# A gated state-space scan on one core: both SiLU gates moved to ScalarE's Silu table, once per unit

## The chip, the cores and the metric

One core of one Trainium2 chip runs the whole program in one launch. The metric is the device time of an execution in microseconds (us). The core has five engines with in-order streams that meet at semaphores: TensorE (PE), VectorE (DVE), ScalarE (ACT), GpSimd (POOL) and SyncE (SP), which here issues the DMAs.

## What is computed

The input is an image batch (4, 512, 24, 24). After a norm over channels it is pixel-shuffled to sequences of 2304 tokens of 128 channels, a token in front, and passed through one selective state-space block. The result is added to the input; then a token norm and a routed mixture of memory tokens follow. The part that matters here:

```python
xz = einsum('bld,ed->ble', seq, in_proj_w);  u, z = split(xz, 2)
u = sum(up[:, k:k + L, :] * conv_w[:, k] for k in range(4)) + conv_b
u = silu(u)
dt, Bm, Cm = split(u @ x_proj_w.T, ...)
dt = softplus(dt @ dt_proj_w.T + dt_proj_b)
A = -exp(A_log)                       # 256 channels x 16 states
h = exp(dt_t * A) * h + (dt_t * u_t) * B_t      # for each token t
y = sum over states of h * C_t
y = (y + u * D) * silu(z)
out = y @ out_proj_w.T
```

All in float32. There are two SiLU gates: that of `u` behind the convolution, and that of `z`, which multiplies the output of the scan.

## The kernel before

Channels of the block (256) lie on 128 partitions in two halves. The sequence is cut into 6 chunks for each of 4 images: 24 **units** of 384 tokens, taken in the order chunk, image. A unit J goes through 16 **steps** `s`, one for each state of the scan. The main work of step s, spread over four engines, is

- ACT, `decay` (L525): `exp(dt * A)` for state s + 1, one activation for each half, from `DT` into the PSUM banks `DA`, where it waits until the scan of state s has read the same half (`scan_done`). There is one such pair of banks, so a decay is computed one state ahead at most;
- DVE, `drive` (L1094), for state s + 1: `dt * u * B`, or POOL in its place (L459) for states 3, 5, 7 and 9, issued two steps ahead; then the two scans of state s (L1130);
- POOL (L447): the product of state s - 1 with C;
- PE (L804): the sum over states into `Yp`, three steps behind.

Round this main work every engine has side work put at fixed steps, for the neighbouring units: in step s of unit J there is work of unit J + 1 (`front`: conv output, `U`, x_proj, softplus) and of unit J - 1 (`back`: gate `VV`, out_proj, residual, token norm, store). The order in each engine's stream is just the order of the code. Of that side work these lines matter:

- **The gate of u**, before. It is computed as `x * exp(-ln(1 + exp(-x)))`, so that all of ScalarE's functions lie in one table set, loaded once (L496): Exp of half 0 in step 15 (L535), Exp of half 1 in step 0 (L539), a clamp on POOL in step 0 (L452), Ln in step 1 (L581), Exp in step 2 (L584), and the product with the PSUM value on DVE in step 3 (L1119), which writes `U`.
- **The gate of z**, before. Exp and a copy out of PSUM (L628, L630), a clamp on POOL in step 13 (L468), Ln and Exp in steps 14 and 15 (L675, L678), and on POOL in step 1 of the next unit the product with z (L438), which writes `GZ`.
- **`VV`** (L1105), DVE, in step 3 before the drive and the scan: `Yp * GZ` of unit J - 1. PE's sum of state 0 of unit J waits for it, since it writes `Yp` anew.
- Behind it on PE, in order: that sum (step 3), x_proj (L816, step 3), in step 4 the spread of B, the next sum, out_proj (L829), the residual (L832) and a small correction (L952). ScalarE copies from these: `PART` and `XDT` (L556, L558) in step 4 ahead of the decays of state 5; `X` and `PART` (L543, L547) in step 5 ahead of the decays of state 6.

In the last three units the routing of the mixture, its gathers and its matmuls (L885) stand in further steps; their weights, eight 128 x 128 blocks for each image, lie in buffers that are free by then.

Of the kernel before, what the change touches and what calls it, by code (L numbers as in the profile page):

```python
# [69 lines left out]
def build(nc, x, tok, w_in, conv_w, conv_b, xp_w, dt_w, dt_b, a_log, dvec, op_w, mem, router, out):  # L70
    ctx = ExitStack()
    with ctx:
# [422 lines left out]
        def _(act):  # L495
# [31 lines left out]

            def step(J, par, s, main, front, back, prev, conv, norm):
# [163 lines left out]
            def prologue():  # L692
# [4 lines left out]
                act.wait_ge(conv_ready, 1)  # L697
                act.activation(SG[:, 0], PP[:, 0, 0:T], ACT.Exp, bias=NCB[:, 0:1], scale=-1.0).then_inc(gate_exp, 1)
                act.wait_ge(gate_clamped, 1)
                act.activation(SG[:, 0], SG[:, 0], ACT.Ln, bias=1.0).then_inc(gate_chain, 1)  # L700
                act.wait_ge(gate_chain, 1)
                act.activation(SG[:, 0], SG[:, 0], ACT.Exp, scale=-1.0).then_inc(gate_ready, 1)

                act.wait_ge(conv_ready, 2)
                act.activation(SG[:, 1], PP[:, 1, 0:T], ACT.Exp, bias=NCB[:, 1:2], scale=-1.0).then_inc(gate_exp, 1)
                act.wait_ge(clamped, 1)
# [573 lines left out]
```

## Time and profile before

| | |
|---|---|
| median of 3 runs | 1246.76 us (1246.51 to 1247.19) |
| profiled execution, its own time | 1244.71 us |
| its span | 1242.9 us |
| mean granted TensorE clock | 0.959 |
| busy: PE / DVE / ACT / POOL | 1069.5 / 1106.5 / 872.8 / 1103.8 us |
| scans (L1130, 768) | 728.2 us, 0.997 each |
| products with C (L447, 384) | 692.2 us, 1.820 each |
| sums (L804, 1536 passes) | 583.5 us |
| decays (L525, 768) | 431.7 us, 0.577 each |

Busy time is what an engine spent in instructions; the rest of the span it waited, and the view of the waits says for whom. A timeline row gives the start, the duration, the engine, the line and what it writes and reads; in brackets stands how long the engine had been idle before it and what ended that. Adjacent instructions of a kind are merged to one row (x2, x4). A granted clock of 1.00 is 2.4 GHz on TensorE; a stretch under that had parts at 1.2 GHz.

### The profile page before, as it was taken

Reading aid. Unit: us, or ns where it says so; the run is one execution under the profiler, and the core shown is the slowest. Engines: PE = TensorE matmul, PEld = TensorE weight load, DVE = VectorE, ACT = ScalarE, POOL = GpSimd, SP = SyncE. Lnnn points to the kernel's source line nnn. Section 1 sums busy time; section 2 is a strip of 40 time slices with the busy share of each in tenths; the row PEclk is TensorE's granted clock in tenths of the full one; section 3 lists DMA queues with packets and bytes.
Section 4 is the critical chain, followed back from the end, with each engine's and each line's share of the span. In section 5 each row is a group of like instructions: output and inputs, shape, how many; then the busy total and the mean of one; then the engine's idle time right before and its main releaser. Section 6 shows DMA issues by size and latency. Waiting matters only on the chain.

```text
span 1242.9 us, 13315 instructions
## 1 busy us (share of the span) xinstructions
PE 1069.5 (86%) x3786; PEld 621.7 (50%) x3786; DVE 1106.5 (89%) x1271; ACT 872.8 (70%) x1629; POOL 1103.8 (89%) x752
## 2 busy tenths in 40 slices
PE   6788888888889889988888898888898988877997
PEld 4455455455455555544554555545555545443454
DVE  3799998989999989999989899999899999978684
ACT  4687676776776876776767768768767777757653
POOL 4589999989999899999998899999998999959685
PEclk9799999899999999999998999999989999989899
DMA  6222132121321222221322213212212222244260
GB/s 170 102 77 103 62 105 94 67 103 60 108 104 59 97 89 77 90 103 59 108 73 88 104 59 108 97 66 91 96 64 104 89 74 102 79 148 171 98 184 26
DMA packets 64540, 116.80 MB, mean 94 GB/s; under 512 B 34219, under 2 KB 47955, under 8 KB 64467
## 3 DMA queue, kind: packets, MB, share of 16 engines
q1 hardware_dynamic: 64466, 115.96, 27.7%
q8 instruction: 30, 0.49, 0.2%
q14 instruction: 44, 0.35, 0.1%
HBM read 108.47 MB, written 7.47 MB: 93 GB/s over the span
## 4 chain that ended last, share of the span: by engine, by line
PE 32%; ACT 23%; DVE 16%; POOL 15%; issue 12%; POOLq 0%; DMA 0%; DVEq 0%; SPq 0%; ACTq 0%
PE Yp L804 13%; DVE SCAN L1130 10%; POOL SCAN L447 7%; ACT DA L525 6%; PE PP L945 5%; POOL SCAN L459 4%; DVE SCAN L1094 3%; PE PP L927 3%; PE PP L885 2%; PE PP L816 2%; ACT GATES L605 2%; ACT GATES L589 1%; ACT GATES L596 1%; ACT GATES L599 1%; ACT GATES L603 1%
## 5 line engine op out<-in xcount | busy, mean ns | idle before, releaser
L1130 DVE TENSOR_TENSOR_SCAN SCAN<-DA,CAR,SCAN 128x384 f32<-128x384 f32 x768 | 728.2, 997 | 50.1 <-ACT DA L525 30.4
L447 POOL TENSOR_TENSOR SCAN<-SCAN,CS 128x768 f32<-128x768 f32 x384 | 692.2, 1820 | 40.1 <-DVE SCAN L1130 39.2
L804 PE MATMUL Yp<-SCAN,IDENT 128*128 128x384 f32 x1536 | 583.5, 506 | 64.9 <-POOL SCAN L447 56.8
L525 ACT ACTIVATE DA<-UDT,A 128x384 f32<-128x384 f32 x768 | 431.7, 577 | 273.1 <-DVE SCAN L1130 271.0
L804 PEld LDWEIGHTS Yp<-SCAN,IDENT 128*128 128x128 f32 x1536 | 285.7, 196 | 261.8 <-POOL SCAN L447 103.9
L1094 DVE TENSOR_TENSOR SCAN<-UDT,BB 128x768 f32<-128x768 f32 x288 | 268.0, 931 | 10.1 <-PE BB L786 10.0
L459 POOL TENSOR_TENSOR SCAN<-UDT,BS 128x768 f32<-128x768 f32 x96 | 175.1, 1824 | 0.0
L945 PE MATMUL PP<-XN,WT 128*128 128x384 f32 x352 | 126.0, 490 | 7.0 <-ACT GZ L630 7.0
L786 PE MATMUL BB<-PT,SEL 96*128 96x384 bf16 x288 | 97.1, 337 | 3.7 <-DVE SCAN L1094 3.7
L945 PEld LDWEIGHTS PP<-XN,WT 128*128 128x128 f32 x352 | 64.8, 189 | 61.0 <-issue 19.9
L475 POOL TENSOR_TENSOR UDT<-UDT 128x768 f32<-128x768 f32 x23 | 41.7, 1813 | 51.9 <-DVE UDT L1177 51.9
L910 PE MATMUL PP<-SQ,MEANW 128*128 128x96 f32 x168 | 28.3, 321 | 45.3 <-ACT SQ L672 45.3
L786 PEld LDWEIGHTS BB<-PT,SEL 96*128 96x128 bf16 x288 | 30.4, 106 | 52.0 <-issue 25.6
L910 PEld LDWEIGHTS PP<-SQ,MEANW 128*128 128x128 f32 x168 | 24.3, 223 | 58.2 <-ACT SQ L672 58.2
L816 PE MATMUL PP<-UDT,XPT 128*104 128x384 f32 x92 | 43.9, 609 | 2.7 <-DVE UDT L1119 2.5
L927 PE MATMUL PP<-XN,WZT 128*128 128x384 f32 x96 | 39.3, 535 | 7.5 <-ACT LNV L620 5.5
L426 POOL TENSOR_TENSOR XN<-XC,RSTD 128x192 f32<-128x192 f32 x48 | 27.0, 587 | 20.7 <-ACT RSTD L690 20.7
L438 POOL TENSOR_TENSOR GZ<-GZ,SGZ 128x768 f32<-128x768 f32 x24 | 43.5, 1814 | 0.7 <-ACT SGZ L678 0.7
L464 POOL TENSOR_TENSOR GATES<-GATES 128x768 f32<-128x768 f32 x23 | 41.8, 1818 | 2.0 <-ACT GATES L610 2.0
L1173 DVE SCALAR_TENSOR_TENSOR GATES<-GATES 128x768 f32<-128x768 f32 x23 | 35.8, 1555 | 4.3 <-ACT GATES L616 4.3
L847 PE MATMUL PP<-SQ,MEANW 128*128 128x96 f32 x192 | 26.4, 280 | 13.7 <-ACT SQ L633 12.8
L829 PE MATMUL PP<-VV,OPT 128*128 128x192 f32 x192 | 36.9, 333 | 1.1 <-DVE VV L1105 1.1
(224 smaller groups left out, 1190.8 us busy)
## 6 DMA issues: line engine op xcount, KB each, us to landing
CS<-bc_rows SPq DMA_DIRECT2D x96, 768.0 KB, 4.1
BS<-bc_rows SPq DMA_DIRECT2D x24, 768.0 KB, 6.0
out<-XN SPq DMA_DIRECT2D x32, 192.0 KB, 2.5
X<-in_x SPq DMA_DIRECT2D x24, 192.0 KB, 3.5
X<-in_L_ffn_memory_tokens SPq DMA_DIRECT2D x16, 256.0 KB, 3.0
XN<-in_L_ffn_memory_tokens SPq DMA_DIRECT2D x16, 256.0 KB, 3.0
bc_rows<-XDT SPq DMA_DIRECT2D x24, 48.0 KB, 1.5
X<-in_L_ffn_memory_router SPq DMA_DIRECT2D x1, 512.0 KB, 3.8
```

The source lines that it names most:

```text
L438: pool.tensor_tensor(GZ[:, :, :], GZ[:, :, :], SGZ[:, :, :], ALU.mult).then_inc(gz_ready, 1)
L447: pool.tensor_tensor(M[:, n1 % MRING], HB[:, n1 % HRING], over_halves(CS[:, n1 % CRING]), ALU.mult).then_inc(m_ready, 1)
L459: pool.tensor_tensor(HB[:, n2 % HRING], DTU[:, par], over_halves(BS[:, pool_index(n2)]), ALU.mult).then_inc(dbu_pool, 1)
L525: act.activation(DA[:, h, 0:T], DT[:, par, h], ACT.Exp, scale=A[:, h, n:n + 1])\
L786: pe.matmul(BB[:, dve_index(n) % 2, 0:T], SEL[:, n], PT[:, par], start=True, stop=True)\
L804: last = pe.matmul(Yp[:, h, 0:T], IDENT[:, :], M[:, n3 % MRING, h], start=n3 == 0, stop=n3 == NS - 1)
L816: last = pe.matmul(PP[0:XROWS, 1, 0:T], XPT[:, h], U[:, fp, h], start=h == 0, stop=h == 1)
L910: last = pe.matmul(STAT, MEANW[:, :], SQ[:, q], start=q == 0, stop=q == Q - 1)
L927: last = pe.matmul(PP[:, h, 0:T], WZT[:, h], unit_seq(J), start=True, stop=True)
L945: last = pe.matmul(PP[:, h, 0:T], WT[:, h, tap], XN[:, ds((J + 2) * SLOT + tap, T)], start=tap == 0, stop=tap == TAPS - 1)
L1094: dve.tensor_tensor(HB[:, n % HRING], DTU[:, par], over_halves(BB[:, dve_index(n) % 2, 0:T]), ALU.mult)\
L1130: dve.tensor_tensor_scan(HB[:, s % HRING, h], DA[:, h, 0:T], HB[:, s % HRING, h], CAR[:, ds(J * NS * HALVES + s * HALVES + h, 1)], ALU.mul ...
```

## The change

Both gates are now one activation each, ScalarE's `Silu`. It lies in another table set than Exp and Ln, so a unit gets one excursion: in step 0, behind the decays of state 0 and ahead of those of state 1, ScalarE loads the set `silu_and_others`, computes `U` of unit J + 1 straight from the convolution's PSUM (two halves, bias in the instruction) and `GZ` of unit J - 1 from a copy `ZB`, and loads the old set again. The z of a unit is copied from PSUM once, at its old place. The clamps, the Ln and Exp passes, the product on POOL and the products on DVE go. The setup does the same once for unit 0. The code also gets a provision for decays computed ahead into SBUF (`AHEAD`, `DAS1`, `DAS2`), but `AHEAD` is the empty tuple, so all decays still go through the one pair of banks. The mixture weights of image 1, which lay in the buffer of the old gates, move to a free part of `XN`; for that ScalarE waits for the stores of the earlier units.

```diff
+AHEAD = ()
@@ step of gpsimd
-                if back and s == 1:
-                    pool.wait_ge(sgz_ready, k + 1)
-                    pool.tensor_tensor(GZ[:, :, :], GZ[:, :, :], SGZ[:, :, :], ALU.mult).then_inc(gz_ready, 1)
...
-                if front and s == 0:
-                    pool.wait_ge(sg_chain, 2 * f + 1)
-                    pool.tensor_scalar(SG[:, :, :], SG[:, :, :], EXP_LIMIT, 0.0, ALU.min, ALU.max).then_inc(clamped, 1)
...
-                if main and s == 13:
-                    pool.wait_ge(sgz_chain, 2 * J + 1)
-                    pool.tensor_scalar(SGZ[:, :, :], SGZ[:, :, :], EXP_LIMIT, 0.0, ALU.min, ALU.max).then_inc(ez_clamped, 1)
@@ step of scalar
-                if conv and s == 15:
-                    act.wait_ge(conv_ready, 2 * (J + 2) + 1)
-                    positive(act, u_ready, J + 2)
-                    act.activation(SG[:, 0], PP[:, 0, 0:T], ACT.Exp, bias=NCB[:, 0:1], scale=-1.0)
-                if front and s == 0:
-                    act.wait_ge(conv_ready, 2 * f + 2)
-                    act.activation(SG[:, 1], PP[:, 1, 0:T], ACT.Exp, bias=NCB[:, 1:2], scale=-1.0).then_inc(sg_chain, 1)
+                if s == 0 and (front or back):
+                    act.preload_act_table_set("silu_and_others")
+                    if front:
+                        act.wait_ge(conv_ready, 2 * f + 1)
+                        positive(act, ysum_done, NS * (f - 2) + 9)
+                        for h in range(HALVES):
+                            act.wait_ge(conv_ready, 2 * f + h + 1)
+                            last = act.activation(U[:, fp, h], PP[:, h, 0:T], ACT.Silu, bias=CB_[:, h:h + 1])
+                        last.then_inc(u_ready, 1)
+                    if back:
+                        act.wait_ge(z_copied, k + 1)
+                        positive(act, v_ready, k)
+                        act.activation(GZ[:, :, :], ZB[:, :, :], ACT.Silu).then_inc(gz_ready, 1)
+                    act.preload_act_table_set("natural_log_exp_and_others")
...
-                if front and s == 1:
-                    act.wait_ge(clamped, f + 1)
-                    act.activation(SG[:, :, :], SG[:, :, :], ACT.Ln, bias=1.0).then_inc(sg_chain, 1)
-                if front and s == 2:
-                    act.wait_ge(sg_chain, 2 * f + 2)
-                    act.activation(SG[:, :, :], SG[:, :, :], ACT.Exp, scale=-1.0).then_inc(sg_ready, 1)
...
-                    positive(act, gz_ready, J)
-                    act.activation(SGZ[:, :, :], PPT, ACT.Exp, scale=-1.0).then_inc(sgz_chain, 1)
-                    positive(act, v_ready, J)
-                    act.activation(GZ[:, :, :], PPT, ACT.Copy).then_inc(z_clamped, 1)
+                    act.activation(ZB[:, :, :], PPT, ACT.Copy).then_inc(z_copied, 1)
...
-                if main and s == 14:
-                    act.wait_ge(ez_clamped, J + 1)
-                    act.activation(SGZ[:, :, :], SGZ[:, :, :], ACT.Ln, bias=1.0).then_inc(sgz_chain, 1)
-                if main and s == 15:
-                    act.wait_ge(sgz_chain, 2 * J + 2)
-                    act.activation(SGZ[:, :, :], SGZ[:, :, :], ACT.Exp, scale=-1.0).then_inc(sgz_ready, 1)
@@ step of vector
-                if front and s == 3:
-                    dve.wait_ge(sg_ready, f + 1)
-                    for h in range(HALVES):
-                        last = dve.scalar_tensor_tensor(out=U[:, fp, h], in0=PP[:, h, 0:T], scalar=CB_[:, h:h + 1],
-                                                        in1=SG[:, h], op0=ALU.add, op1=ALU.mult)
-                    last.then_inc(u_ready, 1)
```

ScalarE, from the z copy of a middle unit to step 3 of the next (`DA` are decays, `SGZ` and `GATES` the old gates), before:

```order
L628 ACTIVATE SGZ<-PP 128x768
L630 ACTIVATE GZ<-PP 128x768
L525 ACTIVATE DA<-UDT,A 128x384 x2
L574 ACTIVATE CAR<-SCAN 128x8
L525 ACTIVATE DA<-UDT,A 128x384 x2
L675 ACTIVATE SGZ<-SGZ 128x768
L535 ACTIVATE GATES<-PP,minus_conv_bias 128x384
L525 ACTIVATE DA<-UDT,A 128x384 x2
L678 ACTIVATE SGZ<-SGZ 128x768
L539 ACTIVATE GATES<-PP,minus_conv_bias 128x384
L525 ACTIVATE DA<-UDT,A 128x384 x4
L574 ACTIVATE CAR<-SCAN 128x8
```

and after the change:

```order
L626 ACTIVATE ZB<-PP 128x768
L513 ACTIVATE DA<-UDT,A 128x384 x2
L579 ACTIVATE CAR<-SCAN 128x8
L513 ACTIVATE DA<-UDT,A 128x384 x4
L529 ACT_TABLE_LOAD
L535 ACTIVATE UDT<-PP,conv_bias 128x384 x2
L540 ACTIVATE GZ<-ZB 128x768
L541 ACT_TABLE_LOAD
L513 ACTIVATE DA<-UDT,A 128x384 x4
L579 ACTIVATE CAR<-SCAN 128x8
```

The side work that stood between several pairs of decays stands in one block between the decays of state 0 (the last two of the first x4) and those of state 1.

GpSimd, from the norm in step 15 to the drive of state 5, before:

```order
L429 COPY XN<-XN 128x3
L447 TENSOR_TENSOR SCAN<-SCAN,CS 128x768
L452 TENSOR_SCALAR GATES<-GATES 128x768
L438 TENSOR_TENSOR GZ<-GZ,SGZ 128x768
L447 TENSOR_TENSOR SCAN<-SCAN,CS 128x768
L459 TENSOR_TENSOR SCAN<-UDT,BS 128x768
L447 TENSOR_TENSOR SCAN<-SCAN,CS 128x768 x2
L459 TENSOR_TENSOR SCAN<-UDT,BS 128x768
```

and after:

```order
L434 COPY XN<-XN 128x3
L448 TENSOR_TENSOR SCAN<-SCAN,CS 128x768 x2
L456 TENSOR_TENSOR SCAN<-UDT,BS 128x768
L448 TENSOR_TENSOR SCAN<-SCAN,CS 128x768 x2
L456 TENSOR_TENSOR SCAN<-UDT,BS 128x768
```

Two operations ahead of the product of state 0 and the drive of state 3 are gone. PE's stream holds the same 1019 rows in both programs, and its order is that of the section above.

## Rows read from the trace of the kernel before

**Rows 1.** The page, busy time of the engines, share of the span, instructions.
```profile
PE 1069.5 (86%) x3786; PEld 621.7 (50%) x3786; DVE 1106.5 (89%) x1271; ACT 872.8 (70%) x1629; POOL 1103.8 (89%) x752
```
**Rows 2.** The waits of VectorE: us in total, times, longest.
```profile
DVE SCAN L1130 <- ACT DA L525: 30.4, 32, 1.1
DVE SCAN L1130 <- POOL SCAN L459: 19.3, 40, 0.7
```
**Rows 3.** Timeline of VectorE, `VV` in units 1 and 20: start, duration.
```profile
96.31 0.92 DVE L1105 TENSOR_TENSOR VV<-Yp,GZ 128x768 f32<-128x768 f32 x1
...
1017.37 0.92 DVE L1105 TENSOR_TENSOR VV<-Yp,GZ 128x768 f32<-128x768 f32 x1
```
**Rows 4.** Timeline of ScalarE and VectorE at the start of unit 20.
```profile
1010.30 0.58 ACT L525 ACTIVATE DA<-UDT,A 128x384 f32<-128x384 f32 x1 [0.26 <-DVE SCAN L1130]
...
1012.29 0.58 ACT L539 ACTIVATE GATES<-PP,minus_conv_bias 128x384 f32<-128x384 f32 x1 [0.64 <-PE PP L945]
1012.77 1.08 ACT L525 ACTIVATE DA<-UDT,A 128x384 f32<-128x384 f32 x2
...
1011.03 1.91 DVE L1130 TENSOR_TENSOR_SCAN SCAN<-DA,CAR,SCAN 128x384 f32<-128x384 f32 x2
...
1013.71 3.73 DVE L1130 TENSOR_TENSOR_SCAN SCAN<-DA,CAR,SCAN 128x384 f32<-128x384 f32 x4
```
**Rows 5.** Groups by line: busy us, mean ns of one, idle before.
```profile
L438 POOL TENSOR_TENSOR GZ<-GZ,SGZ 128x768 f32<-128x768 f32 x24 | 43.5, 1814 | 0.7 <-ACT SGZ L678 0.7
L1119 DVE SCALAR_TENSOR_TENSOR UDT<-PP,conv_bias,GATES 128x384 f32<-128x384 f32 x46 | 26.0, 603 | 0.6 <-ACT GATES L584 0.6
L675 ACT ACTIVATE SGZ<-SGZ 128x768 f32<-128x768 f32 x24 | 19.9, 828 | 0.0
L630 ACT ACTIVATE GZ<-PP 128x768 f32<-128x768 f32 x24 | 19.3, 804 | 0.0
```
**Rows 6.** Timeline of ScalarE at the program's start.
```profile
0.75 1.28 ACT L496 ACT_TABLE_LOAD   x1 [0.75 <-PEq L1269]
11.66 0.52 ACT L683 ACTIVATE SQ<-XC 128x384 f32<-128x384 f32 x1 [9.63 <-DVE XC L1182]
```
**Rows 7.** Timeline of unit 20, steps 3 to 5: VectorE, TensorE, ScalarE.
```profile
1020.44 3.74 DVE L1130 TENSOR_TENSOR_SCAN SCAN<-DA,CAR,SCAN 128x384 f32<-128x384 f32 x4 [0.24 <-POOL SCAN L459]
...
1025.76 3.74 DVE L1130 TENSOR_TENSOR_SCAN SCAN<-DA,CAR,SCAN 128x384 f32<-128x384 f32 x4 [0.73 <-POOL SCAN L459]
...
1018.69 1.56 PE L804 MATMUL Yp<-SCAN,IDENT 128*128 128x384 f32 x4 [2.23 <-POOL SCAN L447]
...
1023.62 1.53 PE L829 MATMUL PP<-VV,OPT 128*128 128x192 f32 x8
...
1025.84 0.49 ACT L543 ACTIVATE X<-PP 128x384 f32<-128x384 f32 x1 [0.97 <-PE PP L832]
```
**Rows 8.** Timeline of unit 12, steps 1 to 6: VectorE, TensorE, ScalarE.
```profile
625.41 3.73 DVE L1130 TENSOR_TENSOR_SCAN SCAN<-DA,CAR,SCAN 128x384 f32<-128x384 f32 x4
...
630.39 1.84 PE L804 MATMUL Yp<-SCAN,IDENT 128*128 128x384 f32 x4 [2.79 <-POOL SCAN L447]
...
632.03 2.80 PE L816 MATMUL PP<-UDT,XPT 128*104 128x384 f32 x4
...
639.22 1.08 ACT L525 ACTIVATE DA<-UDT,A 128x384 f32<-128x384 f32 x2
639.92 1.93 DVE L1130 TENSOR_TENSOR_SCAN SCAN<-DA,CAR,SCAN 128x384 f32<-128x384 f32 x2 [0.55 <-ACT DA L525]
```
**Rows 9.** Busy us by stretch, then the granted clock, DMA share and GB/s.
```profile
581.00:629.00 48.00, 41.73 (x152) 23.78 (x152) 45.07 (x51) 35.28 (x66) 45.45 (x31) 1.00 0.24 88
629.00:678.00 49.00, 43.53 (x152) 25.35 (x152) 45.48 (x53) 35.54 (x66) 45.73 (x31) 0.93 0.25 86
```
**Rows 10.** Timeline of VectorE in units 0 and 23.
```profile
48.09 3.73 DVE L1130 TENSOR_TENSOR_SCAN SCAN<-DA,CAR,SCAN 128x384 f32<-128x384 f32 x4
...
1185.90 0.96 DVE L1105 TENSOR_TENSOR VV<-Yp,GZ 128x768 f32<-128x768 f32 x1 [2.77 <-PE Yp L804]
```

More of the change, by code:

```diff
@@ L33 @@
 XP_M = XROWS
-NEG_LIMIT = -44.0
-EXP_LIMIT = 1.0e19
+AHEAD = ()
 EPS_C, EPS_T = 1e-6, 1e-5
@@ L63, in dve_index, with da_index @@
     return sum(1 for m in range(n) if m not in POOL_STATES)
+def da_index(unit, n):
+    return (NS - len(AHEAD)) * unit + (n - sum(1 for m in AHEAD if m < n))
 def pool_index(n):
@@ L96, in build @@
         GATES = sb("GATES", [P, 4 * HALVES * T])
-        SG, SE, SR, SS = (GATES[:, i * HALVES * T:(i + 1) * HALVES * T].rearrange("p (h t) -> p h t", h=HALVES)
-                          for i in range(4))
-        SGZ = sb("SGZ", [P, HALVES, T])
+        DAS1, SE, SR, SS = (GATES[:, i * HALVES * T:(i + 1) * HALVES * T].rearrange("p (h t) -> p h t", h=HALVES)
+                            for i in range(4))
+        ZB = sb("ZB", [P, HALVES, T])
+        DAS2 = sb("DAS2", [P, HALVES, T])
         GZ = sb("GZ", [P, HALVES, T])
@@ L140, in build @@
         WI = ([WT[:, i // TAPS, i % TAPS] for i in range(TOPK)],
-              [GATES[:, i * P:(i + 1) * P] for i in range(6)] + [X[:, XFREE + i * P:XFREE + (i + 1) * P] for i in range(2)],
+              [XN[:, NFREE + i * P:NFREE + (i + 1) * P] for i in range(6)] + [X[:, XFREE + i * P:XFREE + (i + 1) * P] for i in range(2)],
               [GATES[:, (8 + i) * P:(9 + i) * P] for i in range(TOPK)],
@@ L526, in decay, with decay_ahead @@
                     .then_inc(da_ready, 1)
+            def decay_ahead(J, par, i):
+                n = AHEAD[i]
+                positive(act, scan_done, 2 * (NS * (J - 1) + n + 1))
+                for h in range(HALVES):
+                    act.activation((DAS1, DAS2)[i][:, h], DT[:, par, h], ACT.Exp, scale=A[:, h, n:n + 1])\
+                        .then_inc(das_ready, 1)
             def step(J, par, s, main, front, back, prev, conv, norm):
@@ L563, in step @@
                         unit, upar, n1 = J + 1, 1 - par, 0
-                    if s < NS - 1 or front:
+                    if (s < NS - 1 or front) and n1 not in AHEAD:
                         if n1 == 0:
@@ L568, in step @@
                         decay(unit, upar, n1, N + 1, 1)
+                    if front and s >= NS - len(AHEAD):
+                        act.wait_ge(dt_ready, J + 2)
+                        decay_ahead(J + 1, 1 - par, s - NS + len(AHEAD))
                 if s % GRP == 1 and (main and s > 1 or prev and s == 1):
@@ L655, in step @@
                         act.wait_ge(f_dve, 9)
+                        if b == 1:
+                            act.wait_ge(stored, 16 * (UNITS - 3))
                         if b >= 2:
@@ L695, in prologue @@
                 weights()
[L697 to L706, printed above, removed]
-                act.activation(SG[:, 1], SG[:, 1], ACT.Ln, bias=1.0).then_inc(sg_chain, 2)
-                act.wait_ge(sg_chain, 2)
-                act.activation(SG[:, 1], SG[:, 1], ACT.Exp, scale=-1.0).then_inc(sg_ready, 1)
-                act.wait_ge(set_dve, 3)
-                act.activation(TSG, TUC, ACT.Exp, scale=-1.0).then_inc(set_act, 1)
-                act.wait_ge(set_act, 5)
-                act.activation(TSG, TSG, ACT.Ln, bias=1.0).then_inc(set_act, 1)
-                act.wait_ge(set_act, 6)
-                act.activation(TSG, TSG, ACT.Exp, scale=-1.0).then_inc(set_act, 1)
+                act.preload_act_table_set("silu_and_others")
+                for h in range(HALVES):
+                    act.wait_ge(conv_ready, h + 1)
+                    act.activation(U[:, 0, h], PP[:, h, 0:T], ACT.Silu, bias=CB_[:, h:h + 1])\
+                        .then_inc(u_ready if h else half_u, 1)
+                act.wait_ge(set_pe, 3)
+                for h in range(HALVES):
+                    last = act.activation(TU[:, h:h + 1], ST0[:, h:h + 1], ACT.Silu, bias=CB_[:, h:h + 1])
+                last.then_inc(set_act, 1)
+                act.preload_act_table_set("natural_log_exp_and_others")
                 square(1)
@@ L767, in first_main @@
                 decay(0, 0, 0, 0, 1)
-                act.wait_ge(conv_ready, 3)
-                act.wait_ge(u_ready, 1)
-                act.activation(SG[:, 0], PP[:, 0, 0:T], ACT.Exp, bias=NCB[:, 0:1], scale=-1.0)
+                for i in range(len(AHEAD)):
+                    decay_ahead(0, 0, i)
             prologue()
@@ L1091, in drive @@
                 positive(dve, m_ready, N - HRING + 1)
+                product = DA[:, :, 0:T] if n in AHEAD else HB[:, n % HRING]
                 dve.wait_ge(car_saved, 4 * BATCH + 4 * unit + (n - HRING) // GRP + 1)
                 dve.wait_ge(b_ready, NDVE * unit + dve_index(n) + 1)
-                dve.tensor_tensor(HB[:, n % HRING], DTU[:, par], over_halves(BB[:, dve_index(n) % 2, 0:T]), ALU.mult)\
+                dve.tensor_tensor(product, DTU[:, par], over_halves(BB[:, dve_index(n) % 2, 0:T]), ALU.mult)\
                     .then_inc(dbu_dve, 1)
@@ L1106, in step @@
                 if main:
-                    if s + 1 < NS and s + 1 not in POOL_STATES:
+                    if s + 1 < NS and s + 1 not in POOL_STATES and s + 1 not in AHEAD:
                         drive(J, par, s + 1, N + 1)
@@ L1128, in step @@
                     for h in range(HALVES):
-                        dve.wait_ge(da_ready, 2 * N + h + 1)
-                        dve.tensor_tensor_scan(HB[:, s % HRING, h], DA[:, h, 0:T], HB[:, s % HRING, h],
+                        if s in AHEAD:
+                            dve.wait_ge(das_ready, HALVES * (len(AHEAD) * J + AHEAD.index(s)) + h + 1)
+                            factor, term = (DAS1, DAS2)[AHEAD.index(s)][:, h], DA[:, h, 0:T]
+                        else:
+                            dve.wait_ge(da_ready, 2 * da_index(J, s) + h + 1)
+                            factor, term = DA[:, h, 0:T], HB[:, s % HRING, h]
+                        dve.tensor_tensor_scan(HB[:, s % HRING, h], factor, term,
                                                CAR[:, ds(J * NS * HALVES + s * HALVES + h, 1)],
                                                ALU.mult, ALU.add).then_inc(scan_done, 1)
+                    if s + 1 in AHEAD:
+                        dve.wait_ge(scan_done, 2 * (N + 1))
+                        drive(J, par, s + 1, N + 1)
                 if at(J, ROUTE) and s == 8:
```

74 lines of the change are left out of this document (29 added, 45 removed).

## The prediction

> **What bounds the kernel now.** I read the page first, then the waits of VectorE, the timeline of a unit, and the clock by stretches. The page shows VectorE (DVE), GpSimd (POOL) and TensorE (PE) all at 86 to 89% [rows 1]: no engine alone is full. The waits of VectorE say what fills the rest: its scans stood 30.4 us for ScalarE's decays and 19.3 us for GpSimd's products [rows 2]. So the limit is a ring in lockstep: decay (ACT), scan (DVE), product with C (POOL), sum (PE). The gate product `VV` comes once per unit; from unit 1 to unit 20 it moves from 96.31 to 1017.37, 19 units of 48.48 us [rows 3].
>
> The place that matters is a unit's first states. ScalarE ends the decays of state 0 at 1010.30 + 0.58 = 1010.88; the last Exp of the old gates starts at 1012.29 (it waits for the convolution); VectorE scans state 0 from 1011.03 and state 1 from 1013.71 without a wait [rows 4]. ScalarE had about 0.2 us to spare: an Exp at 1012.29 delays the next decays to 1012.77 by its spacing of 0.48, and a decay needs 0.70 from its start to the start of its scan (639.22 to 639.92 [rows 8]), which makes 1013.47.
>
> **The change, part by part.**
> *Removed per unit.* ScalarE: the three Exp from PSUM and four SBUF passes of 0.83; GpSimd: the product on `GZ`, 1.81, and two clamps of about 0.83 each (as long as the ScalarE pass of that size); VectorE: two multiplies of `U`, 2 x 0.60, 1.13 with their overlap [rows 5]. GpSimd loses 3.5 us. Only 0.24 + 0.73 us of a full-clock unit's VectorE time were waits for GpSimd [rows 7], so at most 0.97 of it can come back.
>
> *Added: the excursion.* It stands on ScalarE between the decays of states 0 and 1. The decays of state 1 cannot start before its end, and VectorE has only one `drive` to do meanwhile; PSUM holds one pair of decay banks, and `AHEAD` is empty, so nothing is decayed in advance. The one table load in the trace took 1.28 us [rows 6]. Silu has no row; its nearest are Exp from PSUM with a bias, 0.58 with a spacing of 0.48 [rows 4], and an SBUF pass of 768, 0.83 [rows 5]. From 1010.88: load to 1012.16; two Silu at 1012.2 and 1012.7; the z gate 1013.1 to 1014.0; load to 1015.25; decay at 1015.3; scan of state 1 at 1016.0, against 1013.71. **The stall is x = 2.3 us.** Its bounds: 2.1 if the loads overlap their neighbours by the 0.1 that adjacent activations do, and 2.7 if each load also waits for the pipe at both ends by 0.1; I take 2.3, the sum of the rows. What follows a load cannot be read off the trace, because ScalarE then waited 9.6 us for data [rows 6].
>
> By itself, the Trainium skill ("ScalarE: Activation LUTs", What ACT_TABLE_LOAD costs) says a switch of set costs a load of about 1283 ns and a drain of about 1380 ns, 2.66 us together. The load agrees with the row of 1.28; no row here shows a drain. By that rule the stall would be 5.1 us instead of 2.3; it is a rival below.
>
> *What the stall moves.* `VV` starts 3.66 us after the scan of state 1 (1013.71 to 1017.37 [rows 3, 4]) and moves with it. Behind `VV` is a serial chain: PE's sum waits for it, then come the x_proj matmuls, ScalarE's `PART`, out_proj, the residual, ScalarE's copy into `X` (L543), `PART` again, and only then, in ScalarE's order, the decays of state 6. In a unit of full clock this chain was just covered: VectorE scanned states 5 and 6 back to back from 1025.76 (state 6 at 1027.63), after a wait for GpSimd. From scan 1 to scan 6 that is 13.92 us [rows 4, 7]. In a unit where PE ran at half clock, the chain was the limit: scan 6 waited 0.55 for its decay, and the distance was 625.41 to 639.92, 14.51 us [rows 8]. So VectorE's removed 1.13 us and the end of the waits for GpSimd do not pay: VectorE gets to state 6 sooner, at about 11.7 us after scan 1, and waits for the chain. The chain itself loses only the wait for `U`, some 0.1, since its first link is `VV`: 14.4 us at half clock, and 13.2 at full (1025.84 + 1.46 as in the other unit = 1027.30, less 0.27 that PE waited for GpSimd and 0.1, from 1013.71).
>
> *The clock.* PE stood idle 2.23 us ahead of that sum and then kept 2.4 GHz (four passes in 1.56), or 2.79 us and ran at 1.2 GHz (x_proj in 2.80) [rows 7, 8]. Of 16 stretches of about a unit, eight had a granted clock of 1.00 and eight 0.93 to 0.97 [rows 9]. The excursion lengthens this idle time by its 2.3 us, to 4.5 us or more, since the sums ahead of it are not late. I therefore expect the half level in nearly every unit.
>
> *The sum per unit.* With about 7 of 16 units in the slow form, the old distance is 13.92 x 9/16 + 14.51 x 7/16 = 14.2. New: 2.3 + 14.4. The difference is 2.5 us; behind state 6 nothing in ScalarE's, VectorE's or PE's order changes but one pass each in places where VectorE does not wait. 20 units x 2.5 = 50; units 21 and 22, with the same chain, 2.4 each = 5, less 0.7 in unit 22, where PE's mixture waits for the copy of z and one copy of 0.80 instead of two comes first [rows 5]. Unit 0 has no `VV` and no z gate: its excursion ends at 47.2, so scan 1 at 47.9 is not late (48.09 before [rows 10]), and `U` is ready early: -1.5. Unit 23's `VV` waited 2.77 for PE [rows 10] and covers its stall. Setup: `U` is two passes sooner but two loads stand in the way, -0.6; tail -0.5. **Sum: +52 us.** The profiled execution took 1244.71 (span 1242.9), giving 1296.7; the median of the runs is 2.05 above it: **1298.5 us.** ScalarE's own load hardly changes (2.6 us of loads for some 3.2 us of passes, net of the Silus) and hides nothing: it is the position that costs. The free output buffers for the mixture weights and the new wait for stores cost 0: those stores were issued units earlier.
>
> **The rivals.**
> *1. PE keeps its full clock, or mostly.* Then the chain takes 13.2 and a unit costs 2.3 + 13.2 - 14.2 = +1.3: 22 x 1.3 - 3 = +26, 1272 us. For: half the stretches were at 1.00 before. Against: the idle time doubles.
> *2. The switch costs more than the load,* as the drain in the skill's page would have it. As a mechanism of this kernel, ScalarE stays shut 1.38 us more at each of two loads, x = 5.1: 22 x 2.8 = 61 more, 1360 us. For: nothing in the trace excludes it, as the only load had nothing behind it. Against: 1.28 us is its whole row, and adjacent activations here even overlap.
> *3. A longer half-clock stretch.* At full clock the next sum (as long as the 1.56 of the first) and out_proj (1.53) [rows 7] take 3.1 us; at 1.2 GHz they would take twice that. If the half level reaches through half of this in the mean, the chain grows by 1.55: 22 x 1.55 = 34 more, 1333 us.
> *4. Not slower: GpSimd was the bound.* It is the busiest engine with VectorE and sheds 3.5 us per unit. If the decays of state 6 are ready when VectorE arrives (11.7 us after scan 1, so that the chain takes no more), the unit gives back its two waits and `U`: 0.97 + 1.13 + 0.2 = 2.3, exactly the stall. It then depends on the excursion: with x = 2.1 the sum is 22 x -0.2 - 3 = -7, 1240 us; the sign turns at about 2.4 us of stall. Against it stands that the chain behind `VV` takes at least 13.2.
> That the change doesn't do what it says isn't one: the order of the built program shows both loads there in each unit. Only its provision for decays ahead is empty.
>
> **How the numbers follow.** Forecast 0.62; rival 1 (with mixtures) 0.12; rival 2 0.14; rival 3 0.08; rival 4 0.04. The likeliest case with x from 2.1 to 2.7 spans 1294 to 1307. The range takes in rival 1 with its smaller stall (1272 - 4) and most of rival 3, and leaves out rivals 2 and 4: 1266 to 1330. A measurement of this kernel can tell about 0.2%, 2.5 us, from no change. Of rival 4's 0.04, 0.03 is faster and 0.01 the same; all other cases are slower.
>
> **What would show it.** In the new profile: two ACT_TABLE_LOAD of 1.28 per unit and 4.4 us from the first to the next decay; the wait of the scans for ScalarE's decays up from 30 us to well over 100; the wait of the scans for GpSimd's products near zero; units of 51.0 us; granted clock 0.93 in all of them; GpSimd busy near 1020 us. A gap between a load and its neighbour proves rival 2; units of 49.8 with clock 1.00 prove rival 1. Units at or under 48.5 would make it wrong altogether.

## The result, and the profile after

| | before | changed |
|---|---|---|
| median of the runs, us | 1246.63 (1243.98 to 1247.19, 4 runs) | 1302.96 (1302.17 to 1303.11, 4 runs) |
| ratio to before | | 1.045, 95% interval 1.0431 to 1.0469 |
| span of the profiled execution, us | 1242.9 | 1301.3 |
| mean granted clock | 0.959 | 0.909 |

The changed kernel is 56 us slower; the prediction was 1298.5, range 1266 to 1330. The page's busy times, answering to [rows 1]:

```profile
PE 1093.1 (84%) x3786; PEld 650.7 (50%) x3786; DVE 1083.6 (83%) x1220; ACT 873.8 (67%) x1581; POOL 1028.2 (79%) x679
```

The share of every engine fell or stayed. PE's busy time rose by 24 us with the same number of matmuls: more of them ran at 1.2 GHz. VectorE's waits, answering to [rows 2] (us in total, times, longest):

```profile
DVE SCAN L1111 <- ACT DA L513: 113.1, 88, 2.2
DVE SCAN L1076 <- PE BB L767: 23.9, 24, 5.4
```

The wait of the scans for ScalarE's decays went from 30.4 to 113.1 us; their wait for GpSimd's products, 19.3 before, is down to one of 0.7. The second line is a wait for PE's spread of B, which stands behind the sum and x_proj on PE (10.0 us before). The new lines, by groups (busy us and mean ns of one, then idle time before them):

```profile
L529 ACT ACT_TABLE_LOAD x25 | 32.1, 1283 | 0.4
L541 ACT ACT_TABLE_LOAD x25 | 32.1, 1283 | 0.4
L535 ACT ACTIVATE UDT<-PP,conv_bias 128x384 f32<-128x384 f32 x46 | 24.2, 577 | 0.3
L540 ACT ACTIVATE GZ<-ZB 128x768 f32<-128x768 f32 x24 | 20.2, 842 | 0.0
```

The start of unit 13 in the timeline (start, duration, engine, line, operation; in brackets the idle time before it and what ended it), first ScalarE, answering to [rows 4]:

```profile
651.76 0.58 ACT L513 ACTIVATE DA<-UDT,A 128x384 f32<-128x384 f32 x1 [0.26 <-DVE SCAN L1111]
652.36 1.28 ACT L529 ACT_TABLE_LOAD   x1
653.66 1.05 ACT L535 ACTIVATE UDT<-PP,conv_bias 128x384 f32<-128x384 f32 x2
654.60 0.84 ACT L540 ACTIVATE GZ<-ZB 128x768 f32<-128x768 f32 x1
655.46 1.28 ACT L541 ACT_TABLE_LOAD   x1
656.75 1.09 ACT L513 ACTIVATE DA<-UDT,A 128x384 f32<-128x384 f32 x2
```

From the first load to the decays of state 1 it is 4.39 us, with 0.02 between a load and its neighbours. On VectorE, and then on PE, answering to [rows 4, 7, 8]:

```profile
652.49 1.92 DVE L1111 TENSOR_TENSOR_SCAN SCAN<-DA,CAR,SCAN 128x384 f32<-128x384 f32 x2
654.32 0.93 DVE L1076 TENSOR_TENSOR SCAN<-UDT,BB 128x768 f32<-128x768 f32 x1
657.47 3.74 DVE L1111 TENSOR_TENSOR_SCAN SCAN<-DA,CAR,SCAN 128x384 f32<-128x384 f32 x4 [2.22 <-ACT DA L513]
661.13 0.93 DVE L1087 TENSOR_TENSOR VV<-Yp,GZ 128x768 f32<-128x768 f32 x1
...
672.04 1.92 DVE L1111 TENSOR_TENSOR_SCAN SCAN<-DA,CAR,SCAN 128x384 f32<-128x384 f32 x2 [1.42 <-ACT DA L513]
```

```profile
662.21 2.90 PE L785 MATMUL Yp<-SCAN,IDENT 128*128 128x384 f32 x4 [4.73 <-DVE VV L1087]
664.90 2.16 PE L797 MATMUL PP<-UDT,XPT 128*104 128x384 f32 x4
666.90 0.33 PE L767 MATMUL BB<-PT,SEL 96*128 96x384 bf16 x1
667.07 1.45 PE L785 MATMUL Yp<-SCAN,IDENT 128*128 128x384 f32 x4
```

Scan 1 stands 2.22 us (2.3 forecast), PE stands idle 4.73 us ahead of the sum (4.5 forecast) and then takes 2.90 for it, the 1.2 GHz level, where [rows 7] had 1.56. (The sum is two matmuls in the program; each stands as two passes in the trace.) Scan 1 to scan 6 is 657.47 to 672.04, 14.57 us (14.4 forecast). The windows, answering to [rows 9], show it in the granted clock, the number behind POOL's busy time. Ten windows of 50 us, one in every 100 us from 95 to 1045, have 0.90 to 0.93; two of them:

```profile
595.00:645.00 50.00, 42.34 (x149) 25.45 (x148) 43.17 (x49) 34.74 (x62) 41.24 (x27) 0.90 0.24 84
695.00:745.00 50.00, 42.33 (x150) 25.26 (x150) 43.55 (x49) 35.33 (x63) 42.55 (x27) 0.93 0.23 80
```

By stages, from the start of `VV` to the next. The two rows of after are the first `VV` and that of unit 21, answering to [rows 3]:

```profile
98.42 0.93 DVE L1087 TENSOR_TENSOR VV<-Yp,GZ 128x768 f32<-128x768 f32 x1
...
1121.65 0.93 DVE L1087 TENSOR_TENSOR VV<-Yp,GZ 128x768 f32<-128x768 f32 x1
```

Before, the `VV` of unit 21 stood at:

```profile
1065.59 0.92 DVE L1105 TENSOR_TENSOR VV<-Yp,GZ 128x768 f32<-128x768 f32 x1
```

| stretch | before | changed | difference | forecast |
|---|---|---|---|---|
| start to the first `VV` (its stall included) | 96.31 | 98.42 | +2.1 | +0.2 |
| 20 units to the `VV` of unit 21 | 969.28 | 1023.23 | +53.9 | +50 |
| to the `VV` of unit 23 | 120.31 | 122.82 | +2.5 | +1.8 |
| the rest | 57.0 | 56.8 | -0.2 | -0.5 |

(The forecast's terms are shared out by this table's stretches: a unit's stall lies before its `VV`, its chain behind it.)

### The profile page after: what moved, and what is told of

It reads as the page before. It is cut to its first block, busy times and chain, and to the rows that moved or that the text cites. A ratio compares the mean times of both kernels' runs of the same rounds, so it can differ in the third digit from the quotient of the medians.

```text
span 1301.3 us, 13143 instructions
## 1 busy us (share of the span) xinstructions
PE 1093.1 (84%) x3786; PEld 650.7 (50%) x3786; DVE 1083.6 (83%) x1220; ACT 873.8 (67%) x1581; POOL 1028.2 (79%) x679
## 4 chain that ended last, share of the span: by engine, by line
ACT 32%; PE 29%; DVE 25%; issue 10%; POOL 4%; DVEq 0%; DMA 0%; POOLq 0%; SPq 0%; ACTq 0%
DVE SCAN L1111 15%; PE Yp L785 14%; ACT DA L513 8%; DVE SCAN L1076 4%; PE PP L797 3%; POOL SCAN L448 3%; DVE GATES L1157 3%; PE PP L810 3%; PE PP L866 2%; ACT L541 2%; ACT UDT L535 2%; ACT L529 2%; DVE VV L1087 2%; PE PP L818 2%; ACT GATES L604 2%
## 5 line engine op out<-in xcount | busy, mean ns | idle before, releaser
L1111 DVE TENSOR_TENSOR_SCAN SCAN<-DA,CAR,SCAN 128x384 f32<-128x384 f32 x768 | 730.7, 1002 | 113.9 <-ACT DA L513 113.1
L785 PE MATMUL Yp<-SCAN,IDENT 128*128 128x384 f32 x1536 | 613.0, 527 | 112.4 <-DVE VV L1087 107.0
L785 PEld LDWEIGHTS Yp<-SCAN,IDENT 128*128 128x128 f32 x1536 | 300.9, 204 | 302.7 <-POOL SCAN L448 132.6
L797 PE MATMUL PP<-UDT,XPT 128*104 128x384 f32 x92 | 51.9, 709 | 0.0
L891 PEld LDWEIGHTS PP<-SQ,MEANW 128*128 128x128 f32 x168 | 21.4, 198 | 56.5 <-ACT SQ L670 56.5
L797 PEld LDWEIGHTS PP<-UDT,XPT 128*104 128x104 f32 x92 | 26.7, 290 | 30.3 <-issue 30.3
L828 PEld LDWEIGHTS PP<-SQ,MEANW 128*128 128x128 f32 x192 | 23.8, 194 | 30.6 <-issue 27.9
```

Source lines behind the costliest of these rows:

```text
L785: last = pe.matmul(Yp[:, h, 0:T], IDENT[:, :], M[:, n3 % MRING, h], start=n3 == 0, stop=n3 == NS - 1)
L797: last = pe.matmul(PP[0:XROWS, 1, 0:T], XPT[:, h], U[:, fp, h], start=h == 0, stop=h == 1)
L828: last = pe.matmul(STAT2, MEANW[:, :], SQ2[:, q], start=q == 0, stop=q == Q - 1)
L891: last = pe.matmul(STAT, MEANW[:, :], SQ[:, q], start=q == 0, stop=q == Q - 1)
L1111: dve.tensor_tensor_scan(HB[:, s % HRING, h], factor, term, CAR[:, ds(J * NS * HALVES + s * HALVES + h, 1)], ALU.mult, ALU.add).then_inc(s ...
```

## Experiments

Eleven kernels ran, in three groups, each beside the kernel before on the same chip; that had medians of 1247.16, 1246.93 and 1245.85 us. "Unit" is the distance from `VV` to `VV`.

**1. The loads alone, in the kernel before.**

```diff
+                if s == 0 and (front or back):
+                    act.preload_act_table_set("silu_and_others")
+                    act.preload_act_table_set("natural_log_exp_and_others")
```

> The kernel before with nothing changed but the two table loads, issued as a pair in step 0 ahead of the Exp of half 1; both gates stay as they were. Theory (the position of the excursion costs, and the work that it removes elsewhere pays nothing back): the pair shuts ScalarE for 2.56 us, of which some 0.8 was spare, so scan 1 is late by 1.7 to 1.8 us and a unit takes 50.5 us; 22 units make about 1292 us, 11 under the changed kernel, whose stall is longer by 0.5. Rival (the changed kernel's lighter GpSimd and VectorE paid part of its loads back, so the loads cost more than it shows): 1303 us or more here.

1302.22 us (1297.12 to 1302.84), ratio 1.0433 (1.0404 to 1.0462): the rival's number, ten over my theory's. The stall itself was near the forecast, 1.64 for 1.7 to 1.8, but the chain behind `VV` was longer, 654.80 to 669.89, 15.09 us instead of 14.5:

```profile
654.80 3.74 DVE L1133 TENSOR_TENSOR_SCAN SCAN<-DA,CAR,SCAN 128x384 f32<-128x384 f32 x4 [1.64 <-ACT DA L525]
658.46 0.93 DVE L1108 TENSOR_TENSOR VV<-Yp,GZ 128x768 f32<-128x768 f32 x1
...
669.89 1.93 DVE L1133 TENSOR_TENSOR_SCAN SCAN<-DA,CAR,SCAN 128x384 f32<-128x384 f32 x2 [1.07 <-ACT DA L525]
```

```profile
659.54 2.90 PE L807 MATMUL Yp<-SCAN,IDENT 128*128 128x384 f32 x4 [3.68 <-DVE VV L1108]
662.23 2.69 PE L819 MATMUL PP<-UDT,XPT 128*104 128x384 f32 x4
```

Stall and chain together are 16.73 us here and 16.79 in the changed kernel. So the two loads, 2.6 us of an engine that is busy two thirds of the time, cost the kernel before as much as the whole change. The Silus between them add 0.6 of stall, and the chain of the changed kernel is 0.5 shorter. These 0.5 are not work taken off VectorE or GpSimd: the sum starts 1.08 behind `VV` and takes 2.90 in both kernels, x_proj takes 2.69 here and 2.16 there, and from the end of x_proj to scan 6 it is 4.97 here and 4.98 there. The level of 2.4 GHz came back 0.5 sooner; why it did is not shown.

**2. The changed kernel without the loads.** Relu stands for Silu, which changes the values and not the passes.

```diff
-                    act.preload_act_table_set("silu_and_others")
...
-                            last = act.activation(U[:, fp, h], PP[:, h, 0:T], ACT.Silu, bias=CB_[:, h:h + 1])
+                            last = act.activation(U[:, fp, h], PP[:, h, 0:T], ACT.Relu, bias=CB_[:, h:h + 1])
...
-                        act.activation(GZ[:, :, :], ZB[:, :, :], ACT.Silu).then_inc(gz_ready, 1)
-                    act.preload_act_table_set("natural_log_exp_and_others")
+                        act.activation(GZ[:, :, :], ZB[:, :, :], ACT.Relu).then_inc(gz_ready, 1)
```

> The changed kernel without its two loads per unit; the two gates use Relu, which the old set has, so U and GZ hold relu instead of silu (the same passes, operands and places). Theory: scan 1 is late by only 0.5 us, PE's idle time ahead of the sum of state 0 falls from 4.7 to about 2.8 us, so the clock is mixed again; scan 1 to scan 6 takes 13.2 to 14.4 us, a unit 48.0 to 49.2, and the time lies between 1236 and 1262, most likely 1247: near the kernel before. Rival (the removed work on GpSimd and VectorE was the bound, and only the loads hide it): units of 46.5 us, 1205 us.

1228.92 us (1224.64 to 1229.58), ratio 0.9859 (0.9841 to 0.9878): between the two, and below my theory's range of 1236 to 1262. In the changed kernel the loads cost 1302.96 - 1228.92 = 74 us, in the kernel before 55 (experiment 1): without loads the removed work is worth 18 us (1247.16 less 1228.92), with them nothing. The profiled execution was the fastest of the four, 1224.64; in it the units alternate between 46.97 and 48.64 us, by PE's clock:

```profile
616.43 3.74 DVE L1109 TENSOR_TENSOR_SCAN SCAN<-DA,CAR,SCAN 128x384 f32<-128x384 f32 x4
...
630.65 1.93 DVE L1109 TENSOR_TENSOR_SCAN SCAN<-DA,CAR,SCAN 128x384 f32<-128x384 f32 x2 [1.43 <-ACT DA L513]
```

```profile
621.16 2.83 PE L783 MATMUL Yp<-SCAN,IDENT 128*128 128x384 f32 x4 [2.49 <-DVE VV L1085]
...
669.81 1.53 PE L783 MATMUL Yp<-SCAN,IDENT 128*128 128x384 f32 x4 [2.49 <-DVE VV L1085]
```

Two units with the same idle time of 2.49 us, one sum at 1.2 GHz and one at 2.4; scan 1 to scan 6 is 14.22 in the first and 12.53 in the second (the scans start at 665.07 and 677.60). The half level costs 1.67 us in such a unit (48.64 less 46.97), and the chain at full clock is 12.5 us, not the 13.2 that I had from [rows 4, 7]: I took off 0.37 for the waits that go, and 1.1 went. Ahead of the sum, of x_proj and of the next sum, PE no longer waits for GpSimd's products and for VectorE's `U`.

**3. PE kept busy ahead of `VV`.** Matmuls of 128x96 that nothing reads, in the changed kernel; 12 of them, and later 19.

```diff
+                        if front and back:
+                            pe.wait_ge(u_ready, f + 1)
+                            for _ in range(FILL):
+                                pe.matmul(PP[:, 1, 0:TOK], IDENT[:, :], MEANW[:, 0:TOK], start=True, stop=True)
```

> The changed kernel with 12 matmuls of 128x96 (never read) on PE in step 3, ahead of its wait for VV, where it stood idle for 4.7 us. Theory: they fill some 3.1 us of it, the sum of state 0 and x_proj then run at 2.4 GHz (1.56 and 1.54 us instead of 2.90 and 2.16), scan 1 to scan 6 takes 13.2 instead of 14.57 us, and the time falls by 22 x 1.2 to 1.4, to about 1274 us. Rival (the half clock lies beside the path, and the stall at state 1 is all): within 5 us of 1303.

> The changed kernel with 19 of the unread matmuls ahead of the sum instead of 12: 4.45 of the 4.73 us in which PE waits for VV are filled. With 12, an idle time of 1.93 us was left, and 16 of 20 units still had half clock (50.84 against 49.15). If what is left of the idle time decides, all units are 49.15: 1285 - 16 x 1.69 = 1258 us (1252 to 1265), the half-clock share of the loss alone. Rival: the half level comes from elsewhere and stays: 1285.

With 12: 1284.87 us (1281.64 to 1287.45), ratio 1.0298 (1.0275 to 1.0321), between the two. In the profiled execution four of 20 units were 49.14 to 49.17 us, the others 50.83 to 50.86. One of each kind:

```profile
453.89 1.56 PE L790 MATMUL Yp<-SCAN,IDENT 128*128 128x384 f32 x4 [1.93 <-DVE VV L1092]
455.29 1.45 PE L802 MATMUL PP<-UDT,XPT 128*104 128x384 f32 x4
...
655.57 1.65 PE L790 MATMUL Yp<-SCAN,IDENT 128*128 128x384 f32 x4 [1.99 <-DVE VV L1092]
657.01 2.77 PE L802 MATMUL PP<-UDT,XPT 128*104 128x384 f32 x4
```

With 19: 1255.65 us (1254.21 to 1257.23), ratio 1.0071 (1.0048 to 1.0093). All units up to unit 20 are 49.14 to 49.16, with at most 0.91 us of idle time left:

```profile
635.61 3.74 DVE L1116 TENSOR_TENSOR_SCAN SCAN<-DA,CAR,SCAN 128x384 f32<-128x384 f32 x4 [2.22 <-ACT DA L514]
...
648.08 1.93 DVE L1116 TENSOR_TENSOR_SCAN SCAN<-DA,CAR,SCAN 128x384 f32<-128x384 f32 x2 [0.68 <-ACT DA L514]
```

```profile
640.26 1.56 PE L790 MATMUL Yp<-SCAN,IDENT 128*128 128x384 f32 x4 [0.90 <-DVE VV L1092]
641.65 1.45 PE L802 MATMUL PP<-UDT,XPT 128*104 128x384 f32 x4
```

The stall of VectorE is the same in this kernel; only PE's clock differs. Holding it up brings back 47 of the 56 us lost. What the clock costs is 51.16 - 49.15 = 2.0 us a unit in the mean, where my forecast had 14.4 - 13.2 = 1.2. This does not make the stall cheap. Scan 1 to scan 6 is 12.47 us here and was 13.92 in a full-clock unit of the kernel before, so the removed work pays back 1.45 of the stall's 2.22 a unit as long as PE keeps its clock.

**4. x_proj ahead of the sum of state 0 on PE**, so that it no longer stands behind `VV`.

```diff
+                if front and s == 3:
+
+                    pe.wait_ge(u_ready, f + 1)
+                    for h in range(HALVES):
+                        last = pe.matmul(PP[0:XROWS, 1, 0:T], XPT[:, h], U[:, fp, h], start=h == 0, stop=h == 1)
+                    last.then_inc(xp_ready, 1)
                 if main and s >= LAG or prev and s < LAG:
...
-                if front and s == 3:
-
-                    pe.wait_ge(u_ready, f + 1)
...
```

> The changed kernel with x_proj of the next unit ahead of the sum of state 0 on PE, so before the wait for VV. U is ready in step 0 now. Theory (VV, sum, x_proj, out_proj, copies, decays of state 6 is one serial chain): x_proj leaves it, scan 1 to scan 6 falls from 14.57 to 12.6 us at half clock or 11.8 at full, where VectorE itself binds; 1259 or 1242 us, I take 1255. Rival (the chain is not what spaces the scans; the stall at state 1 alone costs): within 5 us of 1303.

1265.25 us (1265.01 to 1269.71), ratio 1.0161 (1.0135 to 1.0187): 38 us less than the changed kernel, 10 over the theory's number and far from the rival's. The stall is unchanged; the distance from scan 1 to scan 6 is now 12.91, or 12.71 in every second unit:

```profile
638.41 3.74 DVE L1111 TENSOR_TENSOR_SCAN SCAN<-DA,CAR,SCAN 128x384 f32<-128x384 f32 x4 [2.22 <-ACT DA L513]
...
651.32 1.93 DVE L1111 TENSOR_TENSOR_SCAN SCAN<-DA,CAR,SCAN 128x384 f32<-128x384 f32 x2 [1.12 <-ACT DA L513]
```

Here too the half level came. In the unit shown, and in every second one (49.6 us), it came one link later, as the theory had not foreseen: the first sum took 1.56, the second 2.76. In the units between (49.4 us) the first sum took 2.90.

**5. Decays in advance.** The changed kernel has the code for it with `AHEAD = ()`; one line fills it.

```diff
-AHEAD = ()
+AHEAD = (1, 2)
```

> The changed kernel with AHEAD = (1,): the decays of state 1 are written to SBUF at the end of the unit before, ahead of the excursion, and the product of state 1 takes the free decay banks after scan 0. The excursion then starts about 1.0 us later (two more decays ahead of it) and ends near 657.7 in unit 13's frame of the changed kernel; scan 1 no longer waits, but the decays of state 2 do, so scan 2 stands 1.2 us instead of scan 1's 2.2. Theory (the stall at the excursion moves VV, and the chain behind VV sets the unit): VV comes 0.9 us sooner per unit, the clock stays at half, 1303 - 22 x 0.9 = 1283 us (1270 to 1290). Rival (the loads cost by what they take from ScalarE, whatever its place): 1300 or more.

> The changed kernel with AHEAD = (1, 2): decays of states 1 and 2 in advance. No scan waits for the excursion; scan 0, product 1, scan 1, product 2, scan 2 run without a gap, and VV comes 2.0 us sooner than in the changed kernel, 0.25 us later than with the loads left out. Theory: 22 x 2.0 = 44 off, 1259 us if PE stays at half clock, and 1240 if about half of the units get the full clock, as they did without the loads, where PE stood 2.49 us; I expect 1240 (1225 to 1262). Rival (the loads cost wherever they stand): 1290 to 1303.

`(1,)`: 1295.59 us (1294.3 to 1300.49), ratio 1.0391 (1.0374 to 1.0408). My 1283 was missed, and so was its range; the rival's 1300 is nearer, but no less missed. The profiled execution was the slowest of the four, 1300.49. In it scan 2 waits 1.28 as forecast, and `VV` comes 0.8 us sooner after the decays of state 0 (650.85 to 660.29, against 650.91 to 661.13 in the changed kernel), but the unit is 51.20, as before:

```profile
658.45 1.92 DVE L1111 TENSOR_TENSOR_SCAN SCAN<-DA,CAR,SCAN 128x384 f32<-128x384 f32 x2 [1.28 <-ACT DA L513]
660.29 0.93 DVE L1087 TENSOR_TENSOR VV<-Yp,GZ 128x768 f32<-128x768 f32 x1
```

```profile
661.37 2.90 PE L785 MATMUL Yp<-SCAN,IDENT 128*128 128x384 f32 x4 [3.97 <-DVE VV L1087]
664.06 2.77 PE L797 MATMUL PP<-UDT,XPT 128*104 128x384 f32 x4
666.62 0.49 PE L767 MATMUL BB<-PT,SEL 96*128 96x384 bf16 x1
```

Nearly the whole of x_proj ran at the half level (2.77, where the changed kernel's took 2.16), and the spread of B in part (0.49 for 0.33). Behind `VV`, PE was through with both after 6.82 us instead of 6.10, which ate the gain. Why the full clock came back later stays open.

`(1, 2)`: 1245.28 us (1243.94 to 1248.36), ratio 0.9991 (0.998 to 1.0002), within the range of 1225 to 1262. No scan waits for the excursion; 58 us are recovered. Of the 20 units up to unit 20, eleven are 47.44 to 47.47 us and nine 49.10 to 50.51. This goes with PE's clock again: the sum took 1.53 in each of the eleven and 2.89 or 2.90 in each of the nine. One of each, with as good as the same idle time:

```profile
582.11 1.53 PE L785 MATMUL Yp<-SCAN,IDENT 128*128 128x384 f32 x4 [2.98 <-DVE VV L1087]
...
629.57 2.90 PE L785 MATMUL Yp<-SCAN,IDENT 128*128 128x384 f32 x4 [2.99 <-DVE VV L1087]
```

The version ties with the kernel before.

**6. Both.** The two diffs above together: `AHEAD` filled, and x_proj early.

> As the one before, and the x_proj matmuls stand ahead of the sum of state 0 on PE. Both parts of the loss are then gone, the stall at scan 1 and the chain behind VV. Theory: 1265 (x_proj early alone) - 44 = 1221 us (1205 to 1240), units of 47.0 to 47.4, faster than the kernel before. Rival (VectorE or GpSimd takes over as the bound as soon as one of the two is mended): no better than with decays in advance alone, 1235 or more.

> AHEAD = (1,) and x_proj early. Theory: 1265 - 22 x 0.9 = 1245 us (1232 to 1255), about as the kernel before. Rival: with x_proj out of the way the stall of 1.2 us at scan 2 is covered by something else, and the time falls to that of the kernel with both states in advance, near 1221.

`(1, 2)`: 1220.86 us (1219.86 to 1223.39), ratio 0.9797 (0.9779 to 0.9815), as forecast. `(1,)`: 1255.87 us (1255.21 to 1257.53), ratio 1.008 (1.0063 to 1.0097), 11 over its number and just outside its range, as its sister in experiment 5 was 13 over. In the first, units 1 to 4 are 46.17 and all later ones up to unit 20 are 47.83 to 47.87, so one thing was left:

**7. Both, and PE kept busy.** Behind the early x_proj:

```diff
                     last.then_inc(xp_ready, 1)
+                    if back:
+                        for _ in range(FILL):
+                            pe.matmul(PP[:, 0, 0:TOK], IDENT[:, :], MEANW[:, 0:TOK], start=True, stop=True)
```

> The version with AHEAD = (1, 2) and x_proj early, and ten matmuls of 128x96 whose result nothing reads behind x_proj on PE, about 2.34 us by the 0.234 of one in the filled kernel before, in the 2.60 us in which PE waits for VV. Without them 17 of 22 units ran 47.86 with a stretch at half clock and four 46.17 at full clock. If the idle time sets the clock, all units come at full clock: 1221 - 16 x 1.69 = 1194 us (1190 to 1205), granted clock 0.99. Rival (the clock falls in spite of the filler, as it did in 16 of 20 units with 12 of them ahead of the sum in the changed kernel): 1221 or, with PE in the way of the sum, up to 1228.

> The same with five of them, 1.17 of the 2.60 us: an idle time of 1.4 us is left. If less idle time gives more units of full clock in proportion: 1194 to 1221, near 1207. If the clock goes by a level of idle time that lies under 1.4 us: 1221; if it lies over: 1194.

With ten: 1195.2 us (1193.0 to 1197.77), ratio 0.9595 (0.9562 to 0.9628). With five: **1191.29 us** (1189.25 to 1195.42), ratio 0.9566 (0.9532 to 0.9601), all units up to unit 20 at 46.16 to 46.19. Five were enough. They took 1.25 us (ten rows in the trace, two for a matmul) and left 0.54 to 0.98 in most units and 1.51 to 1.53 in seven of the 20, all at full clock:

```profile
646.33 1.45 PE L783 MATMUL PP<-UDT,XPT 128*104 128x384 f32 x4
647.62 1.25 PE L787 MATMUL PP<-MEANW,IDENT 128*128 128x96 f32 x10
649.48 1.53 PE L795 MATMUL Yp<-SCAN,IDENT 128*128 128x384 f32 x4 [0.61 <-DVE VV L1091]
...
695.67 1.53 PE L795 MATMUL Yp<-SCAN,IDENT 128*128 128x384 f32 x4 [1.52 <-DVE VV L1091]
```

This version beats both kernels. The same filler in the kernel before was not tried: its convolution still stands in the `PP` banks at that point, and the other banks are being read. How much of the 4.3% that kernel could have had too is therefore open; its half-clock units cost it 0.7 us each, 5 to 6 us in all for eight units.

## Why the prediction was right

- **The stall, 2.3 us:** 2.22 measured. It is the plain sum of two loads, two Silus and one z gate. Rival 2, a drain at each load as the Trainium skill ("ScalarE: Activation LUTs", What ACT_TABLE_LOAD costs) has it, is refuted for this kernel: 0.02 us stand between a load of 1.283 and its neighbours on either side. The load's figure agrees with that page of the Trainium skill; the drain does not show.
- **The chain behind `VV`, 14.4 us at half clock:** 14.57. That it hit so closely is partly luck. I read it from a unit whose sum ran mostly at the full level (1.84, then x_proj 2.80 [rows 8], together 4.64), while the changed kernel has 2.90 and 2.16, together 5.06; against that, the sum now starts 1.08 behind `VV` and not 1.33 as in that unit, which I had not taken off. That the chain, and not VectorE, sets the unit is shown by experiment 4, where one link taken out of it is worth 38 us with the stall unchanged.
- **VectorE's and GpSimd's removed work does not pay:** so it was with PE at half clock, as the comparison in experiment 1 shows. At full clock the step is wrong: the chain is 12.5 us and not 13.2, and without the loads the kernel gains 18 us (experiment 2). Rival 4's idea had this part in it, hidden by the loads. PE too had waited for GpSimd and for `U` in the chain, and there 1.1 us went where I took off 0.37.
- **Half clock in nearly every unit:** yes. Its size was too small in my working, 1.2 us a unit instead of 2.0, since the chain at half clock is 14.57 and at full clock 12.47. So rival 1's time of 1272 was 16 too high: with the clock held up, the changed kernel takes 1255.65. Rival 3's longer stretch did not come in the changed kernel (the level returned within x_proj), but did in experiment 5.
- **Units of 51.0:** 51.16 in the mean. The difference of 2.70 instead of 2.5 over 20 units makes 4 of the 6 us by which the growth of the profiled span, 58.4, exceeds the sum of 52. The median is only 4.5 over the forecast, and that too is luck: I added 2.05 because the old profiled execution lay so much under its median, and the new one lies 0.1 over its own.
- **Setup, -0.6:** wrong sign, it was +1.5. The decays of state 0 start at 44.02, before at 42.48. `U` is indeed ready sooner, but PE ran the setup's matmuls at the half level, and ScalarE's waits for it between 28 and 35 us grew from 1.39 to 3.32. Two rows of the same matmuls, before and after:

```profile
29.14 1.13 PE L980 MATMUL BB<-SQ,MEANW 128*128 128x96 f32 x8
```

```profile
29.20 2.02 PE L961 MATMUL BB<-SQ,MEANW 128*128 128x96 f32 x8
```

- **Unit 0, -1.5:** scan 1 stands at 49.62, before at 48.09, and `VV` comes 48.80 later instead of 48.22. Less the stall of 2.2 that lies in it, unit 0 gained 1.6. Tail: +0.5 instead of -0.5; unit 23: -0.7 instead of 0.

## What to carry to other kernels

A pair of table loads is 2.6 us of closed engine, and it costs by its place: put it where the consumers have their next results in hand, which here took the decays of two states in advance and brought 58 of the 74 us back. When an engine's wait feeds PE, price the stall twice, once as time and once as the clock level of the matmuls behind it; here holding up the clock brought back 47 of the 56 us. Before moving work off an engine, find the serial chain that sets the unit and ask which of its links the change shortens.

## What the runs showed of the hardware beyond that

- Silu costs as much as Exp on ScalarE, within 0.02 us: 0.58 us for 128x384 from PSUM with a bias, 0.84 for 128x768 from SBUF (Exp there 0.83).
- The length of one idle time does not tell PE's level behind it. After 2.49 us PE came back at 2.4 GHz in one unit and at 1.2 in the next, in the same program (experiment 2), and so it did after 2.98 and 2.99 (experiment 5). With 12 fillers, a unit with 1.93 came back at the full level and one with 1.99 at the half. After 4.73 no unit of the changed kernel was as short as the full-clock ones; with 1.53 or less left (19 fillers in experiment 3, five in experiment 7) all units up to unit 20 were.
- At equal idle time the moment at which the level falls moves evenly from unit to unit. With 12 fillers the sum took 2.79, 2.43, 2.08 and 1.73 us in four units running, 1.56 in the next, and then began again at 2.70; in the version `(1, 2)` of experiment 6, with 2.60 us idle in nearly every unit, it took 1.64 in unit 5 and about 0.07 more in each unit after it, up to 2.63 in unit 20. The units were equally long all the same (50.83 to 50.86, and 47.83 to 47.87), apart from the one at 1.56.
- More filler is not better: with ten matmuls, which left 0.40 us, units were 46.15 to 46.54 (one of 46.90), with five 46.16 to 46.19. The runs of the two versions overlap (1193.0 to 1197.77, 1189.25 to 1195.42). Why ten did no better was not followed up.
